# Attention order of a fused transformer block rewritten per pair of units

## The chip, the cores and the metric

The kernel runs on one core of one Trainium2 chip. A core has five engines with a queue each: TensorE (PE, matrix products into the PSUM banks), VectorE (DVE), ScalarE (ACT), GpSimd (POOL) and SyncE (SP, which here only starts DMAs). An engine executes its instructions strictly in the order in which they are written and waits at semaphores for the others. The metric is the device time of one launch in microseconds (us); before the change it was 1404.93 us (median of 3 runs, 1403.07 to 1407.63).

## The reference

Inputs are x of 16 sequences by 256 tokens by 256, four attention weights in four-bit codes with scales, and the weights of 64 experts and of one shared expert. In short:

```python
x = x + LN(attn(LN(x)))          # LN: mean and variance over the 256 features
x = x + LN(ffn(LN(x)))
# attn: q, k, v = h @ w + b, 16 heads of 128; softmax(q k^T / sqrt(128)) v @ wo + bo
# ffn, tokens as (4096, 256): softmax gate over 64 experts, best 3 of 8 groups, top 6 experts,
#   capacity 96 rows per expert, last slot shared; silu(x Wg) * (x Wu) @ Wd per expert,
#   weighted sum, plus the same form with the shared expert
```

## The kernel before, in words

The 4096 tokens are 8 blocks (`bp`) of 512 tokens, two sequences each. A unit `u` is one sequence of one head: 256 units, 32 a block; units 2i and 2i+1 are one pair i (the two sequences of one block under one head), 16 pairs a block. The attention stage is a loop over slots: slot u of an engine runs the pieces that `ORDER` lists for even or odd u, each with a lag, so that ("PV", 4) is the PV product of unit u-4 and ("Q", -2) the Q projection of pair (u+2)/2. Every engine walks the same slots, and between them only semaphores hold.

What happens to a pair: Q and K projections into banks 6 and 7 (`proj_qk`, L927), copied out by ACT (`q_out`, L1157) and DVE (`k_out`, L1299); V projection of one quarter of the V rows into bank 2 (`proj_v`, L942), copied to a high half by ACT (L1164) and a low half by DVE (L1304). For each unit: scores in fp32 (`scores`, L956) into bank 0 or 1, row maximum on DVE (`row_max`, L1324), exp with row sums on ACT (`exp`, L1186), reciprocal on DVE (L1320), scaling on POOL (`norm`, L859), high half on ACT (`p_high`, L1195), low half on POOL (`p_low`, L864), a DMA transpose from SP (`turn_p`, L726, PH to PT), then `pv` (L971) into bank 3, the output's high half on ACT (`o_high`, L1178) and low half on DVE (`o_low`, L1330), and the output projection `proj_o` (WO, L988) accumulating over the 16 heads in banks 4 and 5. P, PH, PT, QK and O have two buffers each; a unit waits for the unit two before it to be read.

Into the slots, at "bg", come background chains: `w_job` prepares the weights during the first 24 slots; the x chain (`x_jobs`) loads and normalises the next block and transposes it over bank 7; the post chain (`post_jobs`) of the block just finished takes the sum out of banks 4 and 5, normalises, adds the residual, stores X and the hidden rows to memory (`store`), computes the router and writes the tokens to the experts' rows by 24 indirect DMAs on POOL (L626). Each chain is a strict sequence (`Chain.step` waits for the step before), spread over slots by numbers in the code. After the attention stage come the shared expert, the 64 experts and the last normalisation, whose order `TAIL_ORDER` gives.

The matmuls with the low half of a weight are left out after slot 32 where all low halves are zero, as here: Q, K, V and WO then take 4 matmuls a piece and not 6.

## Time and profile before

| | us |
|---|---|
| median of 3 runs | 1404.93 |
| profiled execution, device time | 1400.53 |
| its span | 1398.8 |
| PE busy (share) | 1232.7 (88%) |
| DVE busy | 875.7 (63%) |
| ACT busy | 832.7 (60%) |
| POOL busy | 925.7 (66%) |

The page's slices of the span (each digit a busy share in tenths, a slice is 35 us) show the stages:

```profile
PE   3589999899999989989989998999966999999984
DVE  5677657678668767867876876786666322222237
POOL 3577646468886976878788697788855513444554
PEclk9899999999999999999999999999987999999977
```

Slices 2 to 29 are attention, where all engines are busy; from slice 31 on the shared expert and the experts follow. A PE that is shown busy counts the latency of its last matmuls too, so a 9 there is not a full PE: the start times of the pieces tell more.

### The profile page before, as it was taken

What the parts mean: (1) busy time and instruction counts of PE and PEld (TensorE: products, weight loads), DVE (VectorE), ACT (ScalarE), POOL (GpSimd) and SP (SyncE); (2) the same over time, 40 slices, a digit from 0 to 9 for tenths busy, and PEclk for the clock granted to TensorE, in tenths of its full rate; (3) what the DMA queues carried; (4) which work ended last, traced back from release to release, by engine and by line L of the source; (5) the groups of instructions that cost most, each with busy time, mean ns of one, the idle gap of its engine ahead of it and who ended that gap; (6) DMA issues with size and microseconds to landing.
All of it is one profiled execution on the core that took longest, in us unless ns stands there. A gap on an engine that the chain in (4) does not pass through costs nothing.

```text
span 1398.8 us, 25701 instructions
## 1 busy us (share of the span) xinstructions
PE 1232.7 (88%) x7872; PEld 857.2 (61%) x7872; DVE 875.7 (63%) x2413; ACT 832.7 (60%) x2256; POOL 925.7 (66%) x1112
## 2 busy tenths in 40 slices
PE   3589999899999989989989998999966999999984
PEld 1356556576666666656666665666633677778953
DVE  5677657678668767867876876786666322222237
ACT  2476558677777777767677776777744332323413
POOL 3577646468886976878788697788855513444554
PEclk9899999999999999999999999999987999999977
DMA  6467697645655454444435444454434559898683
GB/s 201 101 164 166 168 240 151 167 82 119 128 108 103 85 106 94 83 95 80 93 72 91 91 78 80 82 80 85 80 87 139 162 151 238 224 233 215 133 247 121
DMA packets 364489, 182.70 MB, mean 131 GB/s; under 512 B 287248, under 2 KB 343030, under 8 KB 364352
## 3 DMA queue, kind: packets, MB, share of 16 engines
q1 hardware_dynamic: 344768, 166.18, 51.4%
q0 software_dynamic: 16416, 11.70, 4.7%
q10 hardware_dynamic: 3168, 3.15, 0.7%
q8 instruction: 67, 1.10, 0.3%
q14 instruction: 70, 0.57, 0.1%
HBM read 75.32 MB, written 64.69 MB: 100 GB/s over the span
## 4 chain that ended last, share of the span: by engine, by line
PE 34%; DVE 16%; POOL 16%; DMA 13%; ACT 11%; issue 10%; SPq 0%; ACTq 0%; POOLq 0%; DVEq 0%
DMA Y<-W,wix 7%; PE bank L927 6%; POOL PH L864 5%; POOL P L859 5%; DMA PT<-PH 5%; PE bank L956 5%; ACT P L1186 4%; PE bank L971 4%; POOL BUF L626 4%; PE bank L1033 3%; PE bank L942 3%; PE bank L1090 3%; PE bank L988 2%; PE bank L1049 2%; PE bank L1103 2%
## 5 line engine op out<-in xcount | busy, mean ns | idle before, releaser
L864 POOL TENSOR_TENSOR PH<-P,PH 128x512 f16<-128x512 f32 x256 | 300.3, 1173 | 169.8 <-ACT PH L1195 167.1
L927 PE MATMUL bank<-RB,W 128*128 128x512 f16 x1092 | 282.0, 384 | 17.1 <-DVE RB L377 14.0
L956 PE MATMUL bank<-RB 128*128 128x256 f32 x1024 | 252.2, 388 | 33.7 <-DVE RB L1299 13.1
L859 POOL TENSOR_SCALAR P<-P,rr 128x256 f32<-128x256 f32 x512 | 247.7, 492 | 47.3 <-DVE rr L1320 47.3
L1186 ACT ACTIVATE P<-bank,nm 128x256 f32<-128x256 f32 x512 | 237.9, 475 | 26.2 <-DVE nm L1324 19.1
L626 POOL DMA_INDIRECT BUF<-RT,ix x192 | 201.7, 1051 | 67.9 <-issue 35.7
L971 PE MATMUL bank<-PT,RB 128*128 128x256 f16 x1536 | 213.9, 276 | 33.7 <-DVE O L1330 24.6
L956 PEld LDWEIGHTS bank<-RB 128*128 128x128 f32 x1024 | 184.6, 191 | 70.8 <-issue 22.9
L1195 ACT ACTIVATE PH<-P 128x512 f16<-128x512 f32 x256 | 163.4, 638 | 91.1 <-POOL P L859 52.6
L971 PEld LDWEIGHTS bank<-PT,RB 128*128 128x128 f16 x1536 | 147.2, 99 | 107.8 <-issue 46.1
L1178 ACT ACTIVATE O<-bank,bqk 128x256 f16<-128x256 f32 x256 | 123.2, 481 | 125.0 <-PE bank L971 124.9
L1330 DVE SCALAR_TENSOR_TENSOR O<-bank,bqk,O 128x256 f16<-128x256 f32 x256 | 122.6, 479 | 88.9 <-ACT O L1178 87.5
L1324 DVE TENSOR_REDUCE nm<-bank 128x2 f32<-128x512 f32 x256 | 174.2, 680 | 6.3 <-PE bank L956 6.0
L879 POOL DMA_INDIRECT Y<-W,wix x64 | 90.5, 1414 | 127.6 <-ACT W L1257 75.2
L927 PEld LDWEIGHTS bank<-RB,W 128*128 128x128 f16 x1092 | 107.1, 99 | 96.6 <-DVE RB L377 15.5
L988 PE MATMUL bank<-W,O 128*128 128x256 f16 x1078 | 162.0, 276 | 0.2 <-DVE O L1330 0.2
L942 PE MATMUL bank<-W,RB 128*128 128x512 f16 x548 | 139.5, 380 | 3.0 <-DVE RB L1304 3.0
L988 PEld LDWEIGHTS bank<-W,O 128*128 128x128 f16 x1078 | 106.6, 99 | 40.7 <-DVE O L1330 0.7
L1320 DVE RECIPROCAL rr<-rs 128x2 f32<-128x2 f32 x256 | 41.5, 162 | 122.5 <-ACT P L1186 120.4
L1299 DVE TENSOR_SCALAR RB<-bank,bqk 128x512 f32<-128x512 f32 x128 | 95.5, 746 | 34.9 <-PE bank L927 33.0
L1186 ACT ACTIVATION_READ_ACCUMULATOR P<-bank,nm 128x1 f32 x512 | 106.0, 207 | 0.0
L942 PEld LDWEIGHTS bank<-W,RB 128*128 128x128 f16 x548 | 53.6, 98 | 68.7 <-issue 5.0
(200 smaller groups left out, 1675.0 us busy)
## 6 DMA issues: line engine op xcount, KB each, us to landing
RB<-in_ewT SPq DMA_DIRECT2D x24, 352.0 KB
BUF<-zrow SPq DMA_DIRECT2D x4, 1926.0 KB, 8.8
W<-BUF SPq DMA_DIRECT2D x64, 120.4 KB, 4.1
HT<-in_ewT SPq DMA_DIRECT2D x18, 352.0 KB
HT<-in_wc SPq DMA_DIRECT2D x24, 256.0 KB, 3.6
HT<-in_ws SPq DMA_DIRECT2D x24, 256.0 KB, 4.1
Y<-zrow SPq DMA_DIRECT2D x10, 512.0 KB, 3.1
RB<-in_ewd SPq DMA_DIRECT2D x24, 176.0 KB
```

What stands on the lines that cost most here:

```text
L626: eng.indirect_dma_start(BUF, bass.IndirectOffsetOnAxis(ap=ix[:, rt, t, k:k + 1], axis=0), RT[:, rt, t, :], None, bounds_check=CAP * E - 1 ...
L859: r = eng.tensor_scalar(p, p, rr[:, w % 4, t:t + 1], SP_, ALU.mult, ALU.mult)
L864: eng.tensor_tensor(PH[:, w % 2, 1, :], P[:, w % 2, :], PH[:, w % 2, 0, :], ALU.subtract).then_inc(s["pl"], 1)
L927: r = eng.matmul(bk_[:, :], W[:, m, a, c * 2048 + h * 128:c * 2048 + (h + 1) * 128], XT[:, bp % 2, b, c, :], start=(k == 0), stop=(k == n ...
L942: r = eng.matmul(bV[:, :], XT[:, bp % 2, a, c, t * 128:(t + 1) * 128], W[:, 2, b, c * 2048 + hg * 512:c * 2048 + (hg + 1) * 512], start=(k ...
L956: r = eng.matmul(bS[u % 2][:, t * 256:(t + 1) * 256], QK[:, i % 2, 0, q * 256 + t * 128:q * 256 + (t + 1) * 128], QK[:, i % 2, 1, q * 256: ...
L971: r = eng.matmul(bO[:, 0:256], V[:, i // 4 % 2, a, 2 * q + kc, h % 4 * 128:(h % 4 + 1) * 128], PT[:, u % 2, b, :, kc, :], start=(k == 0), ...
L988: r = eng.matmul(bACC[q][:, t * 256:(t + 1) * 256], O[:, u % 2, a, t * 128:(t + 1) * 128], W[:, 3, b, h * 256:(h + 1) * 256], start=(h == ...
L1178: eng.activation(O[:, w % 2, 0, :], bO[:, 0:256], ACT.Identity, bias=bqk[:, 2, h:h + 1]).then_inc(s["oh"], 1)
L1186: r = eng.activation(P[:, u % 2, t * 256:(t + 1) * 256], bS[u % 2][:, t * 256:(t + 1) * 256], ACT.Exp, bias=nm0[:, u % 4, t:t + 1], accum_ ...
L1195: eng.activation(PH[:, w % 2, 0, :], P[:, w % 2, :], ACT.Copy).then_inc(s["ph"], 1)
L1324: eng.tensor_reduce(nm0[:, u % 4, :], bS[u % 2][:, :].rearrange("p (t k) -> p t k", t=2), AX, ALU.max, negate=True).then_inc(s["mx"], 1)
```

## The change

`ORDER` is a new table, by pairs: on PE both scores of a pair stand first, then Q and K of the next pair, the output projections of both units of the pair two before, V three pairs ahead, and both PV products of the pair before. The other engines follow. The output of a pair is now taken out of one full bank by one ACT and one DVE instruction of 512 columns (before: two of 256 each), and waits and buffers of O are by pair. The background chains no longer sit at whole slots but at a position (slot, index in the slot's list) given by `PLACE`; the statistics and normalisations are cut into single steps, the residual sum on POOL into four of 256 columns, and the stores of X and of the hidden rows into two halves each in different slots. Lags: scores to PV was 4 units, it is 2 and 1.

```diff
 ORDER = {
-    "pe": ([("S", 0), ("S", -1), ("PV", 4), ("Q", -2), ("V", -4), ("WO", 5), ("bg", 0), ("K", -2)],
-           [("PV", 4), ("WO", 5), ("bg", 0)]),
-    "act": ([("bg", 0), ("late", 0)],
-            [("O", 5), ("P", 2), ("exp", 1), ("V", -3), ("Q", -1), ("exp", 0), ("O", 4), ("P", 1), ("bg", 0), ("late", 0)]),
-    "dve": ([("O", 5), ("bg", 0), ("max", 0), ("bg", 0), ("O", 4), ("max", -1), ("recip", 0)],
-            [("bg", 0), ("bg", 0), ("K", -1), ("bg", 0), ("V", -3), ("bg", 0), ("recip", 0), ("bg", 0)]),
+    "pe": ([("S", 0), ("S", -1), ("Q", -2), ("K", -2), ("WO", 4), ("WO", 3), ("V", -6), ("PV", 2), ("PV", 1),
+                ("bg", 0)],
+           [("bg", 0)]),
+    "act": ([("exp", 0), ("bg", 0), ("exp", -1)],
+           [("Q", -1), ("P", 1), ("V", -5), ("P", 0), ("O", 3), ("bg", 0)]),
+    "dve": ([("max", 0), ("O", 4), ("max", -1), ("bg", 0), ("recip", 0), ("bg", 0), ("bg", 0)],
+           [("bg", 0), ("recip", 0), ("K", -1), ("bg", 0), ("V", -5), ("bg", 0)]),
     "pool": ([("bg", 0)],
-             [("P", 2), ("norm", 1), ("bg", 0), ("P", 1), ("norm", 0)]),
-    "sp": ([("bg", 0), ("T", 2)],
-           [("bg", 0), ("T", 2)]),
+           [("norm", 1), ("norm", 0), ("P", 1), ("P", 0), ("bg", 0)]),
+    "sp": ([("bg", 0), ("T", 1)],
+           [("bg", 0), ("T", 1)]),
 }
...
+TURN_X = (11, 13)
+PE_AT = (17, 19, 23, 31)
+STORE_AT = (18, 20)
+KEEP_AT = (22, 24)
...
+PLACE = {
...
+        "pool": ((11, 0), (11, 0), (11, 2), (11, 4), (32, 0), (33, 4), (34, 0), (37, 0), (37, 0), (38, 0),
+                (38, 0), (40, 0), (41, 1), (41, 2), (43, 1), (45, 0), (46, 0), (46, 0), (46, 0), (49, 0), (49,
+                1), (49, 4), (49, 4), (51, 4), (52, 0), (54, 0), (54, 0), (55, 3)),
...
-    def step(self, engine, slot, fn, waits=()):
+    def step(self, engine, slot, fn, waits=(), alone=False):
...
-            eng.wait_ge(self.sem, before)
+            if not alone:
+                eng.wait_ge(self.sem, before)
...
-        O = sb("O", [128, 2, 2, 256], F16)
+        O = sb("O", [128, 2, 512], F16)
...
+            def store(eng, h, n=n):
                 eng.wait_ge(s["po"], n)
+                if bp and h == 0:
+                    eng.wait_ge(s["hd"], 32 * bp)
+                eng.dma_start(rows(Hd, h), RT[:, rt, 2 * h:2 * h + 2, 0:D]).then_inc(s["hd"], 16)
...
-                eng.wait_ge(s["ol"], u)
+                eng.wait_ge(s["ol"], i)
...
-                        r = eng.matmul(bO[:, 0:256],
+                        r = eng.matmul(bO[:, q * 256:(q + 1) * 256],
...
-            def o_high(w):
-                h = w // 2 % NH
-                eng.wait_ge(s["pv"], w + 1)
-                if w >= 2:
-                    eng.wait_ge(s["wo"], w - 1)
-                eng.activation(O[:, w % 2, 0, :], bO[:, 0:256], ACT.Identity, bias=bqk[:, 2, h:h + 1]
+            def o_high(i):
+                h = i % NH
+                eng.wait_ge(s["pv"], 2 * i + 2)
+                if i >= 1:
+                    eng.wait_ge(s["wo"], 2 * i)
+                eng.activation(O[:, 0, :], bO[:, :], ACT.Identity, bias=bqk[:, 2, h:h + 1]
```

On PE, one pair of the steady state (head pair i in the middle of a block) stood so before; bank 0 and 1 are scores, 3 PV, 6 Q, 2 V, 7 K, 4 and 5 the output projections:

```order
L956 MATMUL bank0<-RB 128x256 x2
L956 MATMUL bank1<-RB 128x256 x2
L971 MATMUL bank3<-PT,RB 128x256 x6
L927 MATMUL bank6<-RB,W 128x512 x4
L942 MATMUL bank2<-W,RB 128x512 x4
L988 MATMUL bank5<-W,O 128x256 x4
L927 MATMUL bank7<-RB,W 128x512 x4
L971 MATMUL bank3<-PT,RB 128x256 x6
L988 MATMUL bank4<-W,O 128x256 x4
```

Now, from the same place:

```order
L1029 MATMUL bank0<-RB 128x256 x2
L1029 MATMUL bank1<-RB 128x256 x2
L1000 MATMUL bank6<-RB,W 128x512 x4
L1000 MATMUL bank7<-RB,W 128x512 x4
L1061 MATMUL bank4<-W,O 128x256 x4
L1061 MATMUL bank5<-W,O 128x256 x4
L1015 MATMUL bank2<-W,RB 128x512 x4
L1044 MATMUL bank3<-PT,RB 128x256 x12
```

PV and WO of one unit were interleaved twice with the projections; K stood next to last but two, with one PV and one WO between it and the next pair's scores. Now K is followed by both WO, V and both PV.

On ACT, one pair of the same stretch before (P<-bank is exp, PH the high half of P, O the high half of the output):

```order
L1186 ACTIVATE P,rs<-bank0,nm0 128x256 x2
L1164 ACTIVATE RB<-bank2 128x512
L1157 ACTIVATE RB<-bank6,bqk 128x512
L1186 ACTIVATE P,rs<-bank1,nm0 128x256 x2
L1178 ACTIVATE O<-bank3,bqk 128x256
L1195 ACTIVATE PH<-P 128x512
L1178 ACTIVATE O<-bank3,bqk 128x256
L1195 ACTIVATE PH<-P 128x512
```

Now:

```order
L1259 ACTIVATE P,rs<-bank0,nm0 128x256 x2
L1259 ACTIVATE P,rs<-bank1,nm0 128x256 x2
L1230 ACTIVATE RB<-bank6,bqk 128x512
L1268 ACTIVATE PH<-P 128x512
L1237 ACTIVATE RB<-bank2 128x512
L1268 ACTIVATE PH<-P 128x512
L1251 ACTIVATE O<-bank3,bqk 128x512
```

The two exps stand side by side, and one O instruction of 512 columns takes the place of two of 256.

On POOL, the densest place of the new table (slots 45 to 49 counted from a block's base; P<-P is the scaling, PH its low half, DMA BUF a write of tokens). Before, a run of slots read like this:

```order
L864 TENSOR_TENSOR PH<-P,PH 128x512
L859 TENSOR_SCALAR P<-P,rr 128x256 x2
L626 DMA BUF<-RT,ix 6144x321
L864 TENSOR_TENSOR PH<-P,PH 128x512
L859 TENSOR_SCALAR P<-P,rr 128x256 x2
L626 DMA BUF<-RT,ix 6144x321
```

Now, over three pairs:

```order
L691 DMA BUF<-RT,ix 6144x321
L931 TENSOR_SCALAR P<-P,rr 128x256 x4
L936 TENSOR_TENSOR PH<-P,PH 128x512 x2
L691 DMA BUF<-RT,ix 6144x321 x3
L931 TENSOR_SCALAR P<-P,rr 128x256 x4
L936 TENSOR_TENSOR PH<-P,PH 128x512 x2
L691 DMA BUF<-RT,ix 6144x321
L931 TENSOR_SCALAR P<-P,rr 128x256 x2
L691 DMA BUF<-RT,ix 6144x321
L931 TENSOR_SCALAR P<-P,rr 128x256 x2
L936 TENSOR_TENSOR PH<-P,PH 128x512 x2
L691 DMA BUF<-RT,ix 6144x321 x2
```

Before, one token write stood in every slot, two a pair; now the three pairs have one, three and four (the last two of the four stand behind the low halves).

## Rows read from the trace of the kernel before

**Rows 1.** Busy time by stretch; columns: stretch, length, each engine, clock, DMA.

```profile
37.00:128.00 91.00, 70.41 (x391) 44.61 (x390) 66.70 (x125) 53.96 (x140) 62.04 (x67) 0.92 0.58 142
128.00:201.00 73.00, 66.57 (x403) 43.88 (x401) 41.72 (x81) 42.23 (x117) 41.80 (x54) 1.00 0.85 206
201.00:971.00 770.00, 718.92 (x4476) 488.31 (x4474) 564.70 (x1577) 567.06 (x1613) 595.74 (x774) 0.99 0.51 98
...
1015.00:1036.00 21.00, 11.81 (x79) 7.54 (x78) 13.97 (x33) 10.55 (x23) 14.11 (x17) 0.76 0.32 61
```

**Rows 2.** The same view for L1320 alone, between two of its instructions.

```profile
201.50:971.20 769.70, 33.90 (x209) 0.99 0.50 98
```

**Rows 3.** PE in order of time, one pair: start, length, line, count.

```profile
629.13 0.63 PE L371 MATMUL bank<-ident,RT 128*128 128x128 f32 x4 [0.46 <-DVE RB L1299]
629.60 1.89 PE L956 MATMUL bank<-RB 128*128 128x256 f32 x8
631.33 0.82 PE L971 MATMUL bank<-PT,RB 128*128 128x256 f16 x6
631.98 1.03 PE L927 MATMUL bank<-RB,W 128*128 128x512 f16 x4
632.85 1.03 PE L942 MATMUL bank<-W,RB 128*128 128x512 f16 x4
...
635.66 0.60 PE L988 MATMUL bank<-W,O 128*128 128x256 f16 x4
636.10 1.93 PE L956 MATMUL bank<-RB 128*128 128x256 f32 x8
```

**Rows 4.** PE in order of time where it waits; brackets: idle before, releaser.

```profile
607.65 0.60 PE L988 MATMUL bank<-W,O 128*128 128x256 f16 x4
610.75 1.67 PE L927 MATMUL bank<-RB,W 128*128 128x512 f16 x4 [2.50 <-DVE RB L377]
```

**Rows 5.** Groups by line: count, busy us, mean ns, idle before.

```profile
L864 POOL TENSOR_TENSOR PH<-P,PH 128x512 f16<-128x512 f32 x256 | 300.3, 1173 | 169.8 <-ACT PH L1195 167.1
L859 POOL TENSOR_SCALAR P<-P,rr 128x256 f32<-128x256 f32 x512 | 247.7, 492 | 47.3 <-DVE rr L1320 47.3
L1186 ACT ACTIVATE P<-bank,nm 128x256 f32<-128x256 f32 x512 | 237.9, 475 | 26.2 <-DVE nm L1324 19.1 <-POOL PH L864 7.0
L626 POOL DMA_INDIRECT BUF<-RT,ix x192 | 201.7, 1051 | 67.9 <-issue 35.7 <-DVE W L1352 23.6 <-DVE Ms L631 5.7
L1324 DVE TENSOR_REDUCE nm<-bank 128x2 f32<-128x512 f32 x256 | 174.2, 680 | 6.3 <-PE bank L956 6.0
L1195 ACT ACTIVATE PH<-P 128x512 f16<-128x512 f32 x256 | 163.4, 638 | 91.1 <-POOL P L859 52.6 <-DMA PT<-PH 37.5
L1178 ACT ACTIVATE O<-bank,bqk 128x256 f16<-128x256 f32 x256 | 123.2, 481 | 125.0 <-PE bank L971 124.9
L1330 DVE SCALAR_TENSOR_TENSOR O<-bank,bqk,O 128x256 f16<-128x256 f32 x256 | 122.6, 479 | 88.9 <-ACT O L1178 87.5
L1157 ACT ACTIVATE RB<-bank,bqk 128x512 f32<-128x512 f32 x128 | 89.0, 695 | 2.1 <-PE bank L927 2.1
L1304 DVE SCALAR_TENSOR_TENSOR RB<-bank,RB 128x512 f16<-128x512 f32 x128 | 87.0, 679 | 6.0 <-ACT RB L1164 6.0
L1164 ACT ACTIVATE RB<-bank 128x512 f16<-128x512 f32 x128 | 76.2, 595 | 10.9 <-PE bank L942 10.9
L335 DVE SCALAR_TENSOR_TENSOR nw<-nw 128x4 f32<-128x4 f32 x72 | 29.4, 408 | 0.8
```

**Rows 6.** Chain of waits, landing of transposes: start, length, what.

```profile
617.88 5.80 DMA PT<-PH
...
1017.09 3.04 DMA PT<-PH
```

**Rows 7.** PE in order of time, early, where it waits.

```profile
132.83 0.82 PE L971 MATMUL bank<-PT,RB 128*128 128x256 f16 x6 [1.64 <-DVE O L1330]
```

**Rows 8.** PE in order of time, drain of attention: last output projection.

```profile
1034.20 0.61 PE L988 MATMUL bank<-W,O 128*128 128x256 f16 x4 [0.23 <-DVE O L1330]
```

More of the change, by code:

```diff
@@ L66 @@
 FIRST["V"] = max(FIRST["V"], 3)
+FIRST.update({"O": 0})
 WO_LAG = max(lags("pe", "WO"))
@@ L78, in slot_work @@
     order, part = ORDER[who][u % 2], 0
-    for name, lag in order:
+    for j, (name, lag) in enumerate(order):
         w = u - lag
+        if who in PLACE["x"]:
+            work["at"](u, j)
         if name in FIRST:
@@ L84, in slot_work @@
                 work[name](w // 2)
-        elif name == "late":
-            work[name](u)
         elif name == "bg":
@@ L126, in __init__ @@
         self.tail, self.tails = None, 0
-    def step(self, engine, slot, fn, waits=()):
+    def step(self, engine, slot, fn, waits=(), alone=False):
         before = self.n
         self.n += 1
-        if self.tail is not None and slot >= self.tail:
+        if self.tail is not None and slot in (self.tail, self.tail + 101):
             slot = self.tail + self.tails
@@ L340, in normal @@
-        def normal(ch, which, slot, dst, src, waits=()):
-            y, b = NW[which][:, 1, :], NW[which][:, 3, :]
-            yield ch.step("dve", slot, lambda e: e.scalar_tensor_tensor(out=b, in0=MV[which][:, :, 0], scalar=-1.0, in1=y,
-                                                                 op0=ALU.mult, op1=ALU.mult))
-            def f(tiles):
-                def run(eng):
-                    for t in tiles:
-                        r = eng.activation(dst(t), src(t), ACT.Identity, bias=NW[which][:, 3, t:t + 1],
-                                           scale=NW[which][:, 1, t:t + 1])
-                    return r
-                return run
-            if slot < 0 or slot >= END:
-                yield ch.step("act", slot, f(range(4)), waits)
-            else:
-                yield ch.step("act_late", slot, f((0, 1)), waits)
-                yield ch.step("act_late", slot + 1, f((2, 3)))
+            if at is whole:
+                yield ch.step("dve", at("dve"), bns, waits)
+            else:
+                for t in range(4):
+                    yield ch.step("dve", at("dve"), bn(t), () if t else waits, alone=t > 0)
@@ new lines, in normal, with one, four @@
+        def normal(ch, which, at, dst, src, waits=()):
+            y, b = NW[which][:, 1, :], NW[which][:, 3, :]
+            yield ch.step("dve", at("dve"), lambda e: e.scalar_tensor_tensor(out=b, in0=MV[which][:, :, 0], scalar=-1.0,
+                                                                       in1=y, op0=ALU.mult, op1=ALU.mult))
+            def one(t):
+                return lambda eng: eng.activation(dst(t), src(t), ACT.Identity, bias=NW[which][:, 3, t:t + 1],
+                                                  scale=NW[which][:, 1, t:t + 1])
+            def four(eng):
+                for t in range(4):
+                    r = one(t)(eng)
+                return r
+            if at is whole or at is first:
+                yield ch.step("act", at("act"), four, waits)
+            else:
+                for t in range(4):
+                    yield ch.step("act", at("act"), one(t), () if t else waits, alone=t > 0)
@@ L360, in put, with whole, first @@
+        def whole(who):
+            return END
+        def first(who):
+            return PRO
         def put(steps, *args):
@@ L366, in build, with turn @@
         p1_busy = {}
-        def turn(ch, slot, src, c, dst, waits=(), wr=()):
+        def turn(ch, slot, at, src, c, dst, waits=(), wr=()):
             def pe(eng):
@@ L513, in post_jobs @@
+            put(normal, PO, 1, at, lambda t: A[:, t, :], lambda t: A[:, t, :])
+            who, n = ("dve", 2) if last else ("pool", 1)
+            for t in range(0, 4, n):
+                PO.step(who, at(who), lambda e, t=t, n=n: e.tensor_tensor(
+                    X[:, g, t:t + n, :], X[:, g, t:t + n, :], A[:, t:t + n, :], ALU.add), alone=not last and t > 0)
             a_free[bp] = PO.n
-            put(stats, PO, 1, [at_(k) for k in (11, 12, 12, 13)], lambda t: X[:, g, t, :])
+            put(stats, PO, 1, at, lambda t: X[:, g, t, :])
```

216 lines of the change are left out of this document (119 added, 97 removed), and 6 rows, old and new, of the table PLACE.

## The prediction

> **What bounds the kernel now.** I read the page's slices first, then the busy time by stretch, then PE in order of time with what ended each idle time, then the groups by line and the chain of waits. The attention loop runs from about 37 to 1035 us. In its long middle, 201 to 971 us, PE is shown busy 719 of 770 us, DVE 565, ACT 567 and POOL 596 [rows 1]: PE is the fullest, and no other engine is full. L1320 runs once a unit. Between two of its instructions lie 769.7 us, and the row counts 209 of them with both ends, so 208 intervals or 104 pairs: 7.40 us a pair [rows 2].
>
> What would PE need if it never waited? From the scores at 629.60 to those at 636.10 PE ran one whole pair with no gap: 6.50 us [rows 3]. In it two scores take 1.73, one PV 0.65, V, Q or K 0.87 each, one WO 0.44 (differences of start times; the durations in the rows contain the latency of the last matmul, which the next piece hides). Four transpose pieces a block cost 0.47 each, from 629.13 to 629.60 [rows 3]. The 24 logit matmuls and 14 counting matmuls of 64 columns I put at a quarter of a 256-column PV matmul (0.65/6/4 = 0.027), 1.0 together. So a block of 16 pairs has 2.9 us of background on PE, 0.18 a pair, and PE's floor is 6.68. The loop is 0.72 a pair above it, 75 us over 104 pairs. The gaps have many releasers, as they must where order is the cause: PE sat 2.50 idle before L927 until DVE had L377, and the four matmuls behind that gap took 1.67 and not 1.03 [rows 4, 3], because the granted clock had dropped to the lower level. Early, PV waited 1.64 for DVE's low half of O [rows 7].
>
> **The new order, timed from these rows.** I write down one pair with PE's start at 0 and T the length of a pair. Instructions are placed by the new lists and durations from [rows 3, 5]. A handover costs 0.03 to 0.15, and scores are seen 0.15 after their slot ends.
>
> PE: scores 0 to 1.73, Q to 2.60, K to 3.47, WO twice to 4.35, V to 5.2, PV twice to 6.5.
> DVE: maximum of unit 2i 1.1 to 1.8 (0.68), O low half of the pair two before to 2.5, maximum of 2i+1 to 3.15. Then only small work: reciprocals at 3.2 and 4.3, K out 4.4 to 5.2, V low to about 6.5.
> ACT: exp of 2i 1.85 to 2.8 (two instructions of 0.475), exp of 2i+1 3.2 to 4.15, Q out (0.70) to 4.85, P high of 2i (0.64) to 5.5, V high to 6.1, P high of 2i+1 to 6.8, O high to 7.5.
> POOL: scaling of 2i (two of 0.49, seen as 0.93) 3.35 to 4.3, of 2i+1 4.45 to 5.4, low halves (1.17 each) 5.65 to 6.8 and 6.85 to 8.0.
>
> Does a wait close the ring above 6.5? Scores of the next pair need QK, ready at 5.2, and the exps, ready at 4.15: free by over one us. Before, K was followed by only one PV and one WO, 1.1 us, and DVE's K out had to fit in there; that is the tightest handover of the old order. O low (T+2.5) is ready before WO (T+3.47). PV of 2i+1 is due at T+5.85 = 12.35, and its P leaves POOL at 8.0: 4.35 us for the transpose to land. In the drain it took 3.04; behind the block's two 512 KB stores 5.80, with its wait in the SP queue [rows 6]. So with the usual landing the ring closes with 1.3 us to spare. The steady pair can run at PE's floor, and ACT (5.2 a pair) and DVE (3.8) leave room.
>
> **What remains as stalls.** (a) POOL carries 4.2 of attention a pair plus 1.24 per token write (1.07 and 0.17 issue; mean 1.051 in [rows 5]). The new table puts 1, 3 and 4 writes into successive pairs: 5.4, 7.9 and 9.2 us where 6.5 pass. The excess of 4.1 meets 1.9 of slack before PV, so I charge 2.2 a block. (b) At slot 32 DVE does two router steps ahead of the first maximum and four more, with a fourfold MAX, ahead of O low: five steps of 256 columns near L1330's 0.479 and five short ones that I estimate at a third of L1324's 0.68 for an eighth to a half of its columns, some 3.0 us in one pair, where 1.0 is free before WO: 2.0. (c) Four normalisations on ACT in a row after slot 9 (each of 256 columns, between L1178's 0.481 and L1157's 0.695, 2.4 us against 1.3 free) and the router's exps ahead of a unit's exp: 1.2. Sum 5.4 a block, 0.34 a pair: T = 6.68 + 0.34 = 7.02, so 0.38 less than now. Over 104 pairs: -39.5 us.
>
> **The other parts.** First block (41.5 to 201 us): in its first half weights arrive and DVE works on them; those pieces keep their slots. I take nothing off, between +5 and -8. In the second half PE is shown busy 66.6 of 73 us [rows 1], with PV waiting for O low [rows 7]; the new order has O low two us ahead of need. -4 (0 to -7). Output of a pair in one step: ACT two of 0.481 become one near L1157's 0.695, DVE two of 0.479 one near L1304's 0.679 [rows 5], 0.27 and 0.28 a pair. Neither is PE's limit, so alone it is worth nothing; it pays for part of (b) and (c). Cover gone (ACT last in every pair), it would be worth 28 us. Stores in halves: once a block the transposes behind them landed late; this is inside the 0.72 a pair. V six ahead moves a PE piece that nothing waits for: 0; its bound is that V of a block's first heads needs weights a pair earlier, under 1 us once. The many single chain steps add a semaphore wait each, DVE has 205 us idle in 770 to hide them: 0 to +5.
>
> Drain: the last scores end near 1015 and the last WO near 1034.8 [rows 8], 19.8 us, PE shown busy 11.8 of 21 and the clock 0.76 [rows 1], since PV, O high and O low of one unit alternate in one buffer. New: maximum and exp 2.5, scaling 1.0, high and low half 1.9, landing 3.0, last PV 0.8, O high 0.7, O low 0.7, WO 1.0, handovers 0.8, background of the last but one block about 1.4: 13.8. -6 (0 to -8). The stages behind keep their order and start when the last WO ends, so they move along unchanged.
>
> Sum: -39.5 - 4 - 6 = -49.5 us. Against the profiled execution's 1400.5 that is 1351; the median of before is 4.4 higher, so I forecast 1404.9 - 49.5 = 1355 us, 3.5% less.
>
> **A rule that speaks against it.** L335 works on four elements per partition and still takes 0.408 in the mean [rows 5], where L1324 reads 512 columns in 0.680: most of it is not work. The Trainium skill (SBUF — State Buffer, section "Who interferes with whom") says that GpSimd and VectorE share one pair of ports as an exclusive lock, and that a two-input VectorE operation on SBUF contends with GpSimd's reads. By that rule a denser POOL delays the chain steps, and those that stand right ahead of a maximum delay the exp. From rows: two chains a block with nine such steps each, and a POOL instruction held to its end is up to 1.17 us, so at most 21 us of DVE a block; DVE has (770-565)/104*16 = 31 idle. So it is hidden unless it strikes before a maximum; it is one cause of the first rival.
>
> **Rivals.**
> *A: the short path through POOL becomes the limit.* With the two-unit lag the whole chain scores, maximum, exp, scaling, halves, transpose, PV must fit in T+5.85; before, it had two pairs. Both pairs of buffers then tie the ring: two pairs last 8.0 + L + 0.65, L being the landing. For L = 3.04 this asks T = 5.85, nothing; it decides from L = 4.4 (T = 6.5). With L about 5.5, T = 7.1, plus 0.18 and half the stalls, 7.25 to 7.4. Then the gain is 0 to 16 us in the middle and 8 outside: 1380 to 1400. For it: single landings of 5.80. Against: ACT's high half, which waits for the landing of the unit two before, sat idle for it 37.5 us in the whole run [rows 5], 0.15 a unit.
> *B: slower.* Same mechanism, but the path also grows: bursts of POOL writes and ACT normalisations come in most pairs of a block, landing stays near 5.80 and the 8.0 becomes 9. Then 2T = 9.0 + 5.8 + 0.65 and T = 7.73, +0.18 background = 7.9: 0.5 a pair, +52, less 8 outside: +44, 1449; milder, 1410 to 1430. It decides where 8.0 + L passes 13.8 (T + 0.18 = 7.4). For: POOL is at 77% already and must run 9.2 in one pair. Against: its mean demand is 6.2 a pair.
> *C: PE's floor.* The list positions hide the stalls (a) to (c) too: T = 6.75, -68 in the middle, -5 and -7 outside: 1325.
> *D: nothing.* Waits only change their names, T stays at 7.3 to 7.4: 1398 to 1406 with the small terms lost as well.
>
> **Numbers.** A change under 0.3% (4 us) can't be told from none. Forecast (T 6.85 to 7.2, 1335 to 1378) 0.57; C 0.14; A 0.12; D 0.06; B 0.11. Faster: forecast, C and nearly all of A, 0.83; same: most of D, 0.05; slower: B and the rest of D, 0.12. Range for 8 in 10: 1322 to 1392; what lies above it is B, D and A's slow end.
>
> **What would show it.** Right: the distance of 16 instances of the reciprocal's line falls from 59 us to about 56; PE in order of time shows scores, Q, K, WO, V, PV back to back over most pairs; gaps sit near slots 32 and 46 to 49 of a block and are released by DVE's O low or the transpose; clock 1.00 in the middle; last scores to last WO 13 to 15 us. Wrong: PE idle ahead of PV in most pairs, released by the transpose (A, B), or ahead of scores by exp. If the middle is right and the total not, the weights' stage or the tail has moved, which I took as fixed.

## The result, and the profile after

The kernel after takes 1382.75 us (median of four runs, 1377.07 to 1384.56) and the kernel before, on the same chip, 1404.1 (1403.07 to 1407.63): the ratio is 0.9845 [0.9821, 0.987]. So it is faster by about 21 us, 1.5%. The forecast was 1355: the direction is right and the time lies inside the range, but less than half of the forecast gain came. The spans of the two profiled executions are 1398.8 us before and 1381.8 after, 17.0 apart.

The page of the kernel after, its busy times and slices:

```profile
PE 1223.8 (89%) x7876; PEld 855.4 (62%) x7876; DVE 869.4 (63%) x2285; ACT 826.4 (60%) x2128; POOL 922.2 (67%) x1126
...
PE   3789999999899999989999998998966998989984
...
DVE  5766667677668758777976875777765333223337
...
POOL 3576656568877877887887798688755523444554
PEclk9999999999999999999999999999977999999977
```

Busy time by stretch of the kernel after (stretch, length, PE, PEld, DVE, ACT, POOL, clock, DMA), beside [rows 1]:

```profile
192.00:953.00 761.00, 712.99 (x4492) 488.42 (x4491) 566.23 (x1474) 563.38 (x1505) 592.13 (x788) 1.00 0.50 100
...
997.00:1020.00 23.00, 14.00 (x83) 8.85 (x82) 15.93 (x45) 9.49 (x20) 17.57 (x18) 0.71 0.38 87
```

The middle hardly differs from [rows 1]: 48 us of 761 without PE work where it was 51 of 770. Yet the timetable holds for a pair that nothing disturbs. PE of the kernel after in order of time, to be read against [rows 3]:

```profile
635.58 1.89 PE L1029 MATMUL bank<-RB 128*128 128x256 f32 x8
637.31 1.89 PE L1000 MATMUL bank<-RB,W 128*128 128x512 f16 x8
639.04 1.04 PE L1061 MATMUL bank<-W,O 128*128 128x256 f16 x8
639.91 1.03 PE L1015 MATMUL bank<-W,RB 128*128 128x512 f16 x4
640.78 1.47 PE L1044 MATMUL bank<-PT,RB 128*128 128x256 f16 x12
642.09 1.89 PE L1029 MATMUL bank<-RB 128*128 128x256 f32 x8
```

Scores, Q and K, both WO, V, both PV, and the next scores 6.51 us later with no gap. The low halves of this pair leave POOL 6.6 and 7.75 us after its start, where the timetable said 6.8 and 8.0. But such pairs are few: in blocks 2 to 6, 23 of 80 take less than 6.6 us. From the start times of the first scores of each pair (L956 before, L1029 after) I took the length of every pair and added them up by block of 16 pairs (the last block has 15 such lengths):

| block | 0 | 1 | 2 | 3 | 4 | 5 | 6 | 7 |
|---|---|---|---|---|---|---|---|---|
| before, us | 155.6 | 120.1 | 119.7 | 118.7 | 118.7 | 118.1 | 119.2 | 105.6 |
| after, us | 152.4 | 110.4 | 119.2 | 119.4 | 116.8 | 116.7 | 117.9 | 108.5 |

From first to last scores 975.6 became 961.2: 3.2 less in block 0, 9.7 in block 1, and only 1.5 in the six blocks behind, where the forecast wanted most of its 39.5. So more than half of the 17.0 us comes from block 1. Behind the first block, whose pairs also wait for the weights, block 1 is the only one without token writes (those of a block stand at slots 32 and up of its own count, which are slots 0 to 23 of the second block after it). Inside blocks 2 to 6 the mean pair by slot of its first unit tells the same:

| slot | 0 | 2 | 4 | 6 | 8 | 10 | 12 | 14 | 16 | 18 | 20 | 22 | 24 | 26 | 28 | 30 |
|---|---|---|---|---|---|---|---|---|---|---|---|---|---|---|---|---|
| before | 7.08 | 8.10 | 6.57 | 8.07 | 6.68 | 7.05 | 7.34 | 11.31 | 7.13 | 8.44 | 6.76 | 7.33 | 6.64 | 6.83 | 6.61 | 6.95 |
| after | 7.61 | 6.83 | 7.81 | 6.64 | 6.69 | 8.06 | 7.89 | 6.99 | 8.64 | 8.56 | 7.45 | 7.54 | 7.32 | 6.51 | 6.50 | 6.91 |

The pair at slot 14, 11.3 us before (the idle of [rows 4] lies there), became 7.0; what that gave, slots 4, 10, 16, 20 and 24 took back. At slots 26 and 28, behind the last write, a pair takes 6.5.

What ends PE's waits in the kernel after: its groups by line (count, busy us and mean ns, idle before), then single instructions.

```profile
L1044 PE MATMUL bank<-PT,RB 128*128 128x256 f16 x1536 | 197.7, 274 | 29.8 <-DMA PT<-PH 26.5
...
L1061 PE MATMUL bank<-W,O 128*128 128x256 f16 x1080 | 142.6, 276 | 30.3 <-DVE O L1403 26.8
```

```profile
601.47 1.05 PE L1061 MATMUL bank<-W,O 128*128 128x256 f16 x8 [0.85 <-DVE O L1403]
...
613.00 0.83 PE L1044 MATMUL bank<-PT,RB 128*128 128x256 f16 x6 [1.43 <-DMA PT<-PH]
```

PV now waits for the transposes: in the middle 22.8 us of PE's 48 us of idle time end with a landing (7.0 of 51 before), and 12.5 with DVE's low half of O. The chain of waits of the kernel after has 14 landings between 254 and 907 us, none under 4.1 from issue; its first:

```profile
254.41 4.44 DMA PT<-PH
```

The forecast took 3.04 from the drain [rows 6] and let it start at the end of the low half. Landings picked because PE waited for them are the late ones, so I took all of them: for 84 of the 104 second units (2i+1) in the middle the trace has every semaphore record of the transpose. From the end of the low half to the landing they take 4.04 us in the mean and 3.77 in the median, from 3.05 to 7.00; 0.40 of the mean pass before SP starts the transpose, behind the one of the first unit. And in blocks 2 to 6 the low half itself leaves POOL 9.18 us after the start of its pair in the mean, not 8.0, for what stands ahead of it on POOL, ACT and DVE. From landing to PV, 57 of the 84 have less than 1 us, and 31 less than 0.2. Even with POOL at 8.0, 8.0 + 4.04 = 12.04 against the T + 5.85 = 12.35 in which PV is due leaves 0.3 of the forecast 1.3. The slack is small, though not nothing: at slots 26 and 28, with no write and no long step ahead, PE runs without a gap.

### The profile page after: what moved, and what is told of

Read it like the earlier page. It is cut to its first block, busy times and chain, and to the rows that moved or that the text cites. A ratio compares the mean times of both kernels' runs of the same rounds, so it can differ in the third digit from the quotient of the medians.

```text
span 1381.8 us, 25355 instructions
## 1 busy us (share of the span) xinstructions
PE 1223.8 (89%) x7876; PEld 855.4 (62%) x7876; DVE 869.4 (63%) x2285; ACT 826.4 (60%) x2128; POOL 922.2 (67%) x1126
## 3 DMA queue, kind: packets, MB, share of 16 engines
q0 software_dynamic: 16416, 11.70, 4.6%
## 4 chain that ended last, share of the span: by engine, by line
PE 40%; DVE 20%; DMA 13%; POOL 12%; issue 7%; ACT 5%; SPq 2%; another core or an unknown queue 0%; ACTq 0%; POOLq 0%; DVEq 0%
PE bank L1029 7%; PE bank L1000 6%; PE bank L1044 6%; DMA PT<-PH 5%; DMA Y<-W,wix 5%; POOL P L931 4%; POOL PH L936 4%; PE bank L1015 4%; DVE nm L1397 3%; PE bank L1061 3%; PE bank L1163 3%; PE bank L1106 3%; PE bank L1176 2%; PE bank L1122 2%; POOL BUF L691 2%
## 5 line engine op out<-in xcount | busy, mean ns | idle before, releaser
L1000 PE MATMUL bank<-RB,W 128*128 128x512 f16 x1092 | 261.0, 382 | 12.4 <-ACT Sx L620 4.1
L691 POOL DMA_INDIRECT BUF<-RT,ix x192 | 198.3, 1033 | 96.3 <-issue 40.9
L1029 PE MATMUL bank<-RB 128*128 128x256 f32 x1024 | 246.4, 384 | 2.9 <-ACT RB L1230 1.7
L1044 PE MATMUL bank<-PT,RB 128*128 128x256 f16 x1536 | 197.7, 274 | 29.8 <-DMA PT<-PH 26.5
L1397 DVE TENSOR_REDUCE nm<-bank 128x2 f32<-128x512 f32 x256 | 174.3, 681 | 53.8 <-PE bank L1029 53.3
L1029 PEld LDWEIGHTS bank<-RB 128*128 128x128 f32 x1024 | 186.4, 192 | 26.5 <-issue 2.7
L1061 PE MATMUL bank<-W,O 128*128 128x256 f16 x1080 | 142.6, 276 | 30.3 <-DVE O L1403 26.8
L1377 DVE SCALAR_TENSOR_TENSOR RB<-bank,RB 128x512 f16<-128x512 f32 x128 | 87.9, 687 | 93.1 <-ACT RB L1237 85.7
L1259 ACT ACTIVATION_READ_ACCUMULATOR P<-bank,nm 128x1 f32 x512 | 101.1, 197 | 0.0
L1403 DVE SCALAR_TENSOR_TENSOR O<-bank,bqk,O 128x512 f16<-128x512 f32 x128 | 94.8, 740 | 3.6 <-issue 3.2
L1251 ACT ACTIVATE O<-bank,bqk 128x512 f16<-128x512 f32 x128 | 87.4, 683 | 14.6 <-PE bank L1044 8.4
L1230 ACT ACTIVATE RB<-bank,bqk 128x512 f32<-128x512 f32 x128 | 87.9, 687 | 3.0 <-PE bank L1000 3.0
```

Source lines behind the costliest of these rows:

```text
L691: eng.indirect_dma_start(BUF, bass.IndirectOffsetOnAxis(ap=ix[:, rt, t, k:k + 1], axis=0), RT[:, rt, t, :], None, bounds_check=CAP * E - 1 ...
L1000: r = eng.matmul(bk_[:, :], W[:, m, a, c * 2048 + h * 128:c * 2048 + (h + 1) * 128], XT[:, bp % 2, b, c, :], start=(k == 0), stop=(k == n ...
L1029: r = eng.matmul(bS[u % 2][:, t * 256:(t + 1) * 256], QK[:, i % 2, 0, q * 256 + t * 128:q * 256 + (t + 1) * 128], QK[:, i % 2, 1, q * 256: ...
L1044: r = eng.matmul(bO[:, q * 256:(q + 1) * 256], V[:, i // 4 % 2, a, 2 * q + kc, h % 4 * 128:(h % 4 + 1) * 128], PT[:, u % 2, b, :, kc, :], ...
L1061: r = eng.matmul(bACC[q][:, t * 256:(t + 1) * 256], O[:, a, q * 256 + t * 128:q * 256 + (t + 1) * 128], W[:, 3, b, h * 256:(h + 1) * 256], ...
L1259: r = eng.activation(P[:, u % 2, t * 256:(t + 1) * 256], bS[u % 2][:, t * 256:(t + 1) * 256], ACT.Exp, bias=nm0[:, u % 4, t:t + 1], accum_ ...
```

## Experiments

Each block figure is the mean of blocks 2 to 6 of one profiled execution, worked out as above: before 118.9, after 118.0, and 107 is PE's need (16 times 6.50, and 2.9 of background). Two kernels were traced twice and gave 119.7 and 120.5, and 119.1 and 119.5: a difference under 0.8 a block can't be told from none. Ratios are to the kernel before. Edits are cut to the lines that matter.

**Is it the bunching of the token writes?** e1 puts the 24 writes one to a slot, e2 spreads them over 32 slots.

```diff
-        "pool": ((11, 0), (11, 0), (11, 2), (11, 4), (32, 0), (33, 4), (34, 0), (37, 0), (37, 0), (38, 0),
...
+        "pool": ((11, 0), (11, 0), (11, 2), (11, 4)) + tuple(
+            (s, 0 if s % 2 == 0 else 4) for s in range(32, 56)),                            # e1
+            (s, 0 if s % 2 == 0 else 4) for s in (32 + k * 4 // 3 for k in range(24))),     # e2
```

> The changed kernel with the 24 token writes of a block at one per slot (slots 32 to 55, at the bg positions), as in the kernel before, in place of bursts of one to four. In the changed kernel a block whose slots hold no token writes (block 1) takes 110.4 us, the later ones 117 to 119. Theory burst: the bunching costs it; then a block falls to 111-113 us and the total to about 1350-1358 us (1382.8 now). Rival mean load: POOL's two writes a pair cost it wherever they stand; then a block stays at 116-119 us, the total within 4 us of 1383. Rival DVE steps: neither POOL placing matters, also 1383.

> The changed kernel with the 24 token writes spread over 32 slots (three in four slots) instead of 24, evenly. Theory mean load (POOL 4.3 + 2.5 us in each of twelve pairs, above PE's 6.5): at 1.5 writes a pair POOL needs 6.2, under PE's 6.5, a block falls to 111-113 us and the total to about 1350. Theory burst: about the same as the even placing. Rival DVE steps or landings: no change, 1380-1386 us, and the pairs that are slow now (slots 10, 12, 16, 18 of a block) stay slow.

e1: 1375.42 us, 0.9785 [0.9745, 0.9825], block 116.8. e2: 1366.56, 0.9697 [0.9655, 0.974], block 115.2. Neither fell to the 111 to 113 that its theory wanted. The bursts alone cost some 1.2 a block (the two ratios, 0.9785 and 0.9845, just touch in their intervals); thinning out the load helps more (2.8). So it is not only bursts: each write costs.

**What do the writes cost in all, and what in them?** e4 leaves out the writes of blocks 0 to 5, and with them the later waits for their landing. e5 puts in place of each a POOL multiply on scratch memory. e9 issues the writes with a bound that drops nearly every row: the queue of POOL's DMAs moves 0.78 MB in the whole run instead of 11.70, in the same 16416 packets (9504 in e4). e6 is the kernel before, without the same writes.

```diff
                     if last:
                         plan["pool"].setdefault(END + 100, []).append(scatter)
+                    elif bp < 6:
+                        at("pool")                      # e4: nothing is issued
+                        eng.tensor_tensor(scr[:, :], scr[:, :], scr[:, :], ALU.mult)   # e5, 128x432
-                        bounds_check=CAP * E - 1, oob_is_err=False
+                        bounds_check=0 if bp < 6 else CAP * E - 1, oob_is_err=False    # e9
```

> The changed kernel without the token writes of blocks 0 to 5 (the experts' rows of those tokens are left out). Looked at by blocks of 16 pairs in the attention stage, not by its total. Theory POOL writes (time or traffic): blocks 2 to 6 fall from 117-119 to about 110-111 us, like block 1 has now. Rival DVE steps and router steps: they stay at 116-118.

> The changed kernel where each token write of blocks 0 to 5 is replaced at its place by one POOL multiplication of 128x432 on a scratch tile (about 1.0 us, no DMA; those tokens' rows are left out). Blocks 2 to 6 take 118.0 us in the changed kernel and 111.5 without the writes. Theory POOL time: the blocks are at 115.5-118. Rival traffic (the writes' descriptors and bytes delay the transposes): they are at 111-112.5.

> The changed kernel where POOL issues all token writes, but those of blocks 0 to 5 have nearly all rows outside their bound, so that they move almost no bytes (those tokens' rows are missing from the experts). Blocks 2 to 6: 118.0 us in the changed kernel, 111.5 without writes, 113.3 with POOL work of about 1 us in their place. Theory POOL's hold (issue, descriptors, the engine's time): they stay at 116.5-118.5. Rival traffic (bytes delay the transposes): they fall to 112-114.

> The kernel before, without the token writes of blocks 0 to 5. Theory: the old order is bound by its PE and DVE handovers and has slack on the path through POOL, so blocks 2 to 6 (118.9 us) fall by 0 to 2 only, and the change gains some 6 us a block where no writes are and nothing where they are. Rival: the writes cost both orders alike, then they fall by 5 to 7, to 112-114, and the new order has no gain of its own.

One execution each. e4: 1330.91 us, block 111.6, 6.4 less than after. e9: 1377.93, block 116.2: without the bytes only 1.8 of the 6.4 come back, and 4.6 stay with POOL's hold and the packets. e5: 1351.08, block 113.3, which puts back only 1.8, although the 24 multiplies are 21.9 us of POOL. The two stand-ins differ in length (e5's multiply, e9's write; count, busy us and mean ns):

```profile
L702 POOL TENSOR_TENSOR scr<-scr 128x432 f32<-128x432 f32 x144 | 131.4, 912 | 22.4 <-DVE ix L683 15.5
```

```profile
L691 POOL DMA_INDIRECT BUF<-RT,ix x192 | 197.6, 1029 | 93.2 <-issue 36.9
```

POOL's attention work is 4.2 to 4.3 us a pair. Two multiplies of 0.91 fit into 6.5 with it (6.1), two writes of 1.03 with 0.17 of issue do not (6.7). That would explain the difference of 2.8 between e5 and e9, but so would the packets, which e9 still sends and e5 doesn't; no run varied the length, or dropped the packets alone. A third effect is in all of them: DVE steps held beside POOL (below, under the output of a pair). In blocks 2 to 6 nine steps are held for more than 1.2 us beyond their shortest time in the kernel after, five before, four in e5, and none in e4 and e6.

e4 against the kernel after, PE's instructions in the same 761 us:

```profile
192.00:953.00 761.00, 742.60 (x4754) 1.00 0.49 97
```

PE is short of work for 18 us there instead of 48. e6: 1369.21, block 114.1, 4.8 less than before. I had thought that the old order hides the writes behind its longer lag; it doesn't, it pays 4.8 where the new pays 6.4. Without writes the new order is 2.5 a block ahead of the old, with them 0.9, hardly more than two traces of one kernel differ.

**Stores: late, or whole.** e3 moves the halves behind slot 24, where no write stands; e7 and e15 (the same kernel, once with one execution and once with ten) put them back into two whole stores at slot 18.

```diff
-STORE_AT = (18, 20)
-KEEP_AT = (22, 24)
+STORE_AT = (25, 27)      # e3
+KEEP_AT = (29, 31)
-            for h in range(2):
+            plan["sp"].setdefault(base + STORE_AT[0], []).append(lambda e: keep(e, 0))   # e7, e15: 512 rows
```

> The changed kernel with the four half stores moved from slots 18, 20, 22, 24 to 25, 27, 29, 31, where pairs now take 6.50 us. PE waits for a transpose 1.3 us a block at slot 18 and 0.6 at 20. Theory landing: the stores' bytes delay the transposes behind them; then slots 18 to 22 lose 1.5 to 2 us a block and slots 24 to 30, which have slack, gain less: total 6 to 10 us less. Rival POOL path: the transposes are late because POOL hands them over late; then the waits stay at 18 and 20, total within 3 us.

> The changed kernel with this part undone: the stores of a block again in one piece each, both at slot 18. Theory landing: transposes behind 1 MB in one go land later; blocks 1 to 3 (with both stores) lose 1 to 3 us, slot 18's pair above all; blocks 4 to 6 (one store) 0 to 1. Rival: halves are worth nothing, all blocks within 1 us of 110.4 and 118.0.

> The changed kernel with the stores of a block in one piece each at slot 18, this time with its time. One look gave 1389.9 us, and the pair at slot 18 took 10.6 us against 8.6. Theory landing: 1387-1392. Rival: 1381-1385.

e3: 1377.34, 0.979 [0.9755, 0.9824], block 116.2; the pair at slot 18 falls from 8.56 to 7.31 and its wait for the transpose from 1.28 to 0.11. e7: 1389.92. e15: 1395.39, 0.9945 [0.9924, 0.9966], blocks 119.1 and 119.5. The SP queue of e15, and PE behind it:

```profile
617.47 0.57 SPq L589 DMA_DIRECT2D Xd<-X  x1
618.13 0.48 SPq L585 DMA_DIRECT2D Hd<-RT  x1
618.71 5.33 SPq L796 DMA_TRANSPOSE PT<-PH  x2
```

```profile
624.45 1.46 PE L1042 MATMUL bank<-PT,RB 128*128 128x256 f16 x6 [3.33 <-DMA PT<-PH]
```

The pair at slot 18 takes 10.5 us in the mean. Stores in halves over four slots are worth 1.0% in the new order, some 13 us, which the forecast had inside other terms; how much of it is the halving and how much the spreading wasn't separated.

**Output of a pair in one step.** e8 and e14 (the same kernel, once with one execution and once with ten) take O out in two instructions of 256 columns on each engine.

```diff
-                eng.activation(O[:, 0, :], bO[:, :], ACT.Identity, bias=bqk[:, 2, h:h + 1])
+                for q in range(2):
+                    r = eng.activation(O[:, 0, q * 256:(q + 1) * 256], bO[:, q * 256:(q + 1) * 256], ACT.Identity,
+                                       bias=bqk[:, 2, h:h + 1])        # and so on DVE
```

> The changed kernel with a pair's output scaled in two instructions of 256 columns on ACT and two on DVE (this part undone, order kept). Adds 0.27 us to ACT and 0.28 (0.22 by the 740 ns measured) to DVE a pair. By my costing at nothing: blocks 1 and 2 to 6 within 1 us of 110.4 and 118.0. Rival: ACT and DVE are late in the slow pairs, then 2 to 4 us a block more.

> The changed kernel with each pair's output scaled in two instructions of 256 columns again, this time with its time. One look gave 1395.3 us and 119.7 us for blocks 2 to 6 against 118.0. Theory: with no slack on ACT and DVE the merge is worth 6 to 13 us: 1388-1396. Rival, my costing: nothing, 1381-1385.

e8: 1395.34, block 119.7. e14: 1395.18, 0.9952 [0.9922, 0.9982], block 120.5. The groups of e14 (count, busy us and mean ns), each of which is one of half the count in the kernel after (0.683 and 0.740 us):

```profile
L1252 ACT ACTIVATE O<-bank,bqk 128x256 f16<-128x256 f32 x256 | 106.8, 470 | 13.5 <-PE bank L1044 6.8 <-issue 5.9
```

```profile
L1407 DVE SCALAR_TENSOR_TENSOR O<-bank,bqk,O 128x256 f16<-128x256 f32 x256 | 110.8, 474 | 4.3 <-ACT O L1252 4.2
```

So 0.26 of ACT and 0.21 of DVE a pair come with 1.1%, 12 to 15 us. But the price isn't spread over the pairs. Of the 2.5 a block by which e14 is longer, 2.2 lie in the one pair at slot 2: it takes 9.5 to 9.7 us in blocks 2, 3, 5 and 6 and 6.50 in block 4. In these four a background step of 64 columns, ahead of K out on DVE, takes 3.9 us. e14 in block 3, DVE, POOL and PE (the granted clock is 0.52 behind the gap):

```profile
434.86 3.88 DVE L708 TENSOR_TENSOR L<-L,Ls 128x64 f32<-128x64 f32 x1
...
438.74 0.74 DVE L1374 TENSOR_SCALAR RB<-bank,bqk 128x512 f32<-128x512 f32 x1
```

```profile
434.58 1.84 POOL L931 TENSOR_SCALAR P<-P,rr 128x256 f32<-128x256 f32 x4
436.40 2.26 POOL L936 TENSOR_TENSOR PH<-P,PH 128x512 f16<-128x512 f32 x2
```

```profile
439.57 3.57 PE L1029 MATMUL bank<-RB 128*128 128x256 f32 x8 [2.34 <-issue]
```

The step ends when POOL's four scalings and two low halves have ended; K out and with it the next scores come that much later. In the kernel after the same step takes 0.5 in blocks 3 to 6, and the next scores don't wait:

```profile
550.97 0.49 DVE L708 TENSOR_TENSOR L<-L,Ls 128x64 f32<-128x64 f32 x1
```

In e8 it takes 3.9 in three of the five blocks, and there 1.6 of its 1.8 a block lie in that pair. What is left for the longer instructions themselves, 0.2 to 0.3 a block, can't be told from nothing. Why the step is held to POOL's last instruction in four blocks and takes 0.20 in block 4, no run shows. O low ahead of WO is waited for 1.2 us at slot 16, where it was 0.9.

**The new order without the tables of positions.** e16 keeps the new order of pairs, the merged output and the halves, and puts the chain steps at whole slots, spread over the slot's free places, about as before. The token writes stand one to a slot in it.

```diff
-        "dve": ((3, 3), (4, 6), (4, 6), (5, 2), (5, 3), (6, 0),
+    "p": {"dve": ((3, 3), (4, 5), (6, 3), (6, 5), (6, 5), (6, 6), (6, 6), (7, 0), (7, 3), (7, 3), ...
+          "pool": ((11, 4), (11, 4), (12, 0), (12, 0)) + tuple((s, 0 if s % 2 == 0 else 4) for s in range(34, 58))},
```

> The new order of pairs with the background chains placed at whole slots again, shared out over the bg positions of a slot about as in the kernel before (the O step merged and the stores in halves as in the changed kernel). This leaves of the change mostly the order of pairs. Theory: the order alone makes the fast pairs (6.50 us) and the tables are worth 5 to 15: 1388-1398. Rival: the order alone is worth nothing or less without its tables: 1400-1415.

1462.78 us, 1.0411 [1.0358, 1.0464]: slower than before by 4%, and some 80 us slower than after, though the writes are spread. Nothing that I ran moved the time more. It is one placement of many. PE of e16, DVE in the same place, and PE's busy time with the clock just behind:

```profile
630.19 1.03 PE L985 MATMUL bank<-RB,W 128*128 128x512 f16 x4
635.16 1.86 PE L985 MATMUL bank<-RB,W 128*128 128x512 f16 x4 [3.94 <-DVE RB L414]
```

```profile
631.94 0.16 DVE L360 TENSOR_SCALAR nw<-mv 128x4 f32<-128x4 f32 x1
...
632.73 0.38 DVE L367 SCALAR_TENSOR_TENSOR nw<-nw 128x4 f32<-128x4 f32 x1
633.14 0.63 DVE L364 TENSOR_TENSOR nw<-nw 128x4 f32<-128x4 f32 x1
633.81 0.40 DVE L365 SCALAR_TENSOR_TENSOR nw<-nw 128x4 f32<-128x4 f32 x1
634.24 0.16 DVE L367 SCALAR_TENSOR_TENSOR nw<-nw 128x4 f32<-128x4 f32 x1
634.33 0.69 DVE L414 SCALAR_TENSOR_TENSOR RB<-bank,RB 128x512 f16<-128x512 f32 x1
```

```profile
635.00:638.00 3.00, 2.84 (x10) 0.50 0.00 0
```

K goes through the same bank as the transposed normalised rows, and stands now 2.6 us behind the start of a pair, right after the transposes. DVE runs eight small steps of a chain and a reciprocal before L414 empties the bank, and PE sits 3.94 us; the four matmuls behind take 1.86 and not 1.03, since the granted clock there is 0.50 (last row: the view by stretch, PE), as in [rows 4]. Steps of the router (2.5 at slot 24, logits in the same bank) do the same. This is the wait of the old order's slot 14, in more places: waits of Q and K for DVE's L414 and for the router's steps are 3.9 of e16's 16 us of idle PE a block at slot 14, 2.5 at slot 24, 1.7 each at slots 0 and 12, and 1.9 at 18 and 20 together.

**A version that moves what the traces name.** e10: writes one to a slot in 24 of slots 33 to 63, stores late (e3's slots), the residual sum, the router steps at slot 32 and four normalisations moved out of the way of a maximum, of O low or of an exp. e13 moves one more sum to position (4, 3) and the router's last steps behind slot 33. e11 is e10 with ACT's high halves of P ahead of Q out and V high.

```diff
-        "dve": ((3, 3), (4, 6), (4, 6), (5, 2), (5, 3), (6, 0),
+        "dve": ((3, 3), (3, 5), (4, 6), (5, 2), (5, 3), (6, 0),                          # e10
+        "dve": ((3, 3), (4, 3), (4, 6), (5, 2), (5, 3), (6, 0),                          # e13
-... (32, 0), (32, 0), (32, 1), (32, 1), (32, 1), (32, 1), (33, 1), (33, 1), (34, 1), (35, 0), (35, 2)),
+... (32, 0), (32, 0), (32, 0), (32, 5), (32, 5), (32, 5), (33, 3), (33, 3), (34, 5), (35, 3), (35, 3)),
-(10, 0), (15, 4), (16, 0), (16, 2), (17, 2), (18, 0),                                      # act
+(10, 0), (15, 5), (15, 5), (16, 1), (17, 0), (18, 0),
-[("Q", -1), ("P", 1), ("V", -5), ("P", 0), ("O", 3), ("bg", 0)]
+[("P", 1), ("Q", -1), ("P", 0), ("V", -5), ("O", 3), ("bg", 0)]                            # e11
```

> The changed kernel with four tables moved: token writes in 24 of the slots 33 to 63, one each; residual sums on POOL behind the low halves; stores at 25 to 31; DVE's router steps behind the first reciprocal of slot 32 and the second sum of bank 5 one slot earlier; ACT's RT normalisations behind O. Spread writes alone gave 1366.6 us, late stores alone 1377.3, against 1382.8. Theory zero slack (a transpose lands about 4.4 us after the low half, so each thing put ahead of a unit on POOL, ACT or DVE reaches PE): blocks fall to 111.5-114 and the total to 1345-1358. Rival: the parts overlap and DVE's moves give nothing: 1360-1366.

> As the one before, and on ACT the high half of P of unit 2i stands ahead of Q's copy, and the one of 2i+1 ahead of V's. The low halves start 0.2 us earlier, V low is 0.6 later. Theory zero slack: 0.1 us off each pair that waits for a transpose, -1 to -6 us more than e10. Rival: ACT then idles 0.2 until the scaling is done and V low delays the next maximum: 0 to +8 us.

> The moved kernel (1357.4 us) with DVE's sum of bank 5 at slot 4 between the second maximum and the first reciprocal, not at the end of slot 3, and the last router steps at the ends of slots 33 and 34. There PE waits 1.1 us for O low at slot 4, and that pair takes 8.4 us. Theory zero slack: the pair falls to about 7.2, a block by 1, the total by 4 to 8, to 1350-1354. Rival: the wait only goes to the sum itself or to the exp: 1356-1360.

e10: 1357.42 (1355.12 to 1366.19), 0.968 [0.9644, 0.9716], block 113.6. e13: 1357.87, 0.9677 [0.9623, 0.973], block 113.2: the pair at slot 4 fell from 8.45 to 7.79 and the total stayed. e11: 1367.67, 0.9743 [0.972, 0.9766], block 114.7: 10 us are lost where 1 to 6 were to be won. P earlier means Q out and V high later; scores that wait for Q out at slots 12 and 16 are 0.5 of the 1.1 a block, and the rest I did not trace. PE of e10 in 761 us, against 712.99 in the kernel after:

```profile
192.00:953.00 761.00, 733.28 (x4646) 1.00 0.51 103
```

e10 beats both kernels: 3.2% less than before where the change brought 1.5%. It differs from the kernel after in nothing but positions. Most of it is the spreading of the writes, which e2 has alone at 0.9697: the intervals of the two ratios overlap, so what the other moves add isn't shown by the times, only by the blocks (115.2 and 113.6).

## Why the prediction was right in sign and wrong in size

- **The steady pair.** Right where nothing stands in its way: 6.50 us, POOL's halves on time, clock 1.00. The step that failed is "So with the usual landing the ring closes with 1.3 us to spare". The landing came from the drain, where little else moves, and without the 0.4 us in SP's queue: 3.04 against 4.04 in the loop, which leaves 0.3; and the low half leaves POOL at 9.18 in the mean, not at 8.0, because nothing that stands ahead of it was in the 8.0. The 37.5 us of ACT's high half idle for the landing [rows 5] did not speak against rival A, since that half waits only for the landing of the unit two before.
- **Rival A** named the path, and the time lies between its 1380 and 1400 with T at its 7.25 to 7.4; it got a chance of 0.12. But it needed a landing near 5.5, and "it decides from L = 4.4" is not reached in the mean: with 4.04 its own formula gives T = 6.35, nothing. The path is late in some pairs, for the writes, the held steps and the stores. That A's number came out is in part luck.
- **Stalls (a), the writes.** The term that was mis-sized most: charged 2.2 a block, they cost 6.4, of which some 1.2 is the bunching. That is 4.2 a block, 25 us over the six blocks that have writes, nearly the whole miss of 28. The working took 1.9 of slack, which is the first unit's (11.7 less 6.8 and 3.04), where the second had 1.3 by the same sum; it left out the pairs at slots 40 and 54, which also get three writes; and it gave a pair with two writes no price, though 4.2 + 2.48 is over 6.5.
- **(b) and (c), router steps and normalisations.** The pairs at slots 0 and 2 take 1.4 more than 13.0 (charged 2.0; the five steps of 0.479 and five of 0.23 add up to 3.5 and not 3.0, so it should have been 2.5), the one at slot 10 takes 1.6 more (charged 1.2): near enough, though writes stand there too. PE's wait at slot 24 for the router's exp is 0.61 a block, which the charge has only as a delay of a unit's exp.
- **Sum of the middle.** T was to be 7.02 and is 118.0/16 = 7.38; without the writes it is 111.6/16 = 6.97. Before it was 7.43.
- **The rule that spoke against it.** The forecast put a hold of a small DVE step at up to 1.17 and hid all of them unless one strikes ahead of a maximum. Holds reach 3.4 us in the kernel after and 3.9 in e14. They do strike ahead of a maximum, and ahead of K out. Around 597 us, DVE, then POOL, of the kernel after:

```profile
597.21 1.10 DVE L382 SCALAR_TENSOR_TENSOR nw<-nw 128x4 f32<-128x4 f32 x1
598.34 1.08 DVE L388 SCALAR_TENSOR_TENSOR nw<-mv,nw 128x4 f32<-128x4 f32 x1
...
599.94 0.67 DVE L1397 TENSOR_REDUCE nm<-bank 128x2 f32<-128x512 f32 x1
```

```profile
597.13 2.27 POOL L936 TENSOR_TENSOR PH<-P,PH 128x512 f16<-128x512 f32 x2
```

The two steps of four elements hold up V low (L1377) and the maximum (L1397) on DVE, and on ACT the normalisation that waits for L388 and starts at 599.45, with O high behind it until 600.63. O low comes behind all of them, and WO waits for it the 0.85 us at 601.47 above. What the holds cost in all, no run separates from the writes.
- **Merged output.** "Alone worth nothing": taking it back costs 12 to 15 us by e14, but nearly all of it by way of one held step. For the instructions' own length the zero isn't refuted.
- **Stores in halves.** Put inside other terms; worth some 13 us by e15, and at slot 18 even a half costs 1.3.
- **Chain positions.** Taken for 0 to +5 of semaphore waits. With the placement of e16 the new order is 80 us slower. The working looked at PE's waits on units, not at what the earlier K needs of its bank.
- **Block 1.** Its 9.7 us were no term of the forecast. Most of them are two pairs of the old order: the one at slot 0 took 9.6 us and takes 6.6; the one at slot 18 took 12.1 and takes 8.3, for there the two transposes behind the stores, the second behind five more DMAs too, landed 8.2 and 10.4 us after their low halves, and PE waited 1.36 and 1.53 for them.
- **First block and drain.** Block 0 gave 3.2 (forecast 4). From the last scores' end to the last WO's end 19.8 [rows 8] became 15.6 (1000.3 to 1015.9; forecast 13.8); the stages behind became 1.9 longer and not equal. PE in the drain of the kernel after, with its two long waits for O low:

```profile
998.57 1.89 PE L1029 MATMUL bank<-RB 128*128 128x256 f32 x8
...
1008.01 1.89 PE L1061 MATMUL bank<-W,O 128*128 128x256 f16 x8 [3.64 <-DVE O L1403]
...
1014.03 1.89 PE L1061 MATMUL bank<-W,O 128*128 128x256 f16 x8 [1.57 <-DVE O L1403]
```

What the runs do not settle: the prices of single parts do not add up (e14, e15 and e16 each take one part from the whole, and the three make 12, 13 and 80 us, of a change worth 21), why the old order needs 9.6 us for the first pair of block 1, and how much of the writes' 6.4 is POOL's time, how much the packets and how much the held DVE steps. A lag of V shorter than six wasn't tried.

## What to carry to other kernels

Where the order makes several engines and a transfer follow each other with two buffers, add up that path with every term taken under the loop's own load: the transfer's over all of its instances and not only where its consumer waited, the queue ahead of it, and the work that stands ahead of each engine's part. If little slack is left, as here, busy shares of the engines tell nothing of the price of background work; take away one kind of it and look by block. The price of a part that shifts DVE by tenths of a microsecond has to be looked for pair by pair before it is put down to the part's own length. Whoever moves a producer ahead must list everyone who holds its buffer at the new place.
